# Second attention: a bank of its own for projections, one bank of values by 256 columns, context in quarters

## The reference, cut to what matters

```python
x = x + _L0_xattn_ref(_layernorm(x), ctx_1024, ...)
x = x + _L0_ffn_ref(_layernorm(x), ...)
x = x + _L1_xattn_ref(_layernorm(x), ctx_1024, mask, Wq, Wkv, Wo)   # the stage that changes
x = x + _L1_ffn_ref(_layernorm(x), ...)

def _L1_xattn_ref(x, context, mask, Wq, Wkv, Wo):     # x 4x512x256, context 4x1024x256
    q = (x @ Wq).reshape(B, N, H, D).transpose(0, 2, 1, 3)            # H = 4 heads of D = 64
    kv = (context @ Wkv).reshape(B, M, 2, H, D).transpose(2, 0, 3, 1, 4)
    k, v = (kv[0], kv[1])
    attn = jnp.einsum('bhnd,bhmd->bhnm', q, k) * SCALE
    attn = jnp.where(mask[:, None, :, :], attn, -jnp.inf)
    attn = jax.nn.softmax(attn, axis=-1)
    out = jnp.einsum('bhnm,bhmd->bhnd', attn, v)
    return out.transpose(0, 2, 1, 3).reshape(B, N, C) @ Wo
```

## Time and profile before

| | |
|---|---|
| median of 3 runs | 1119.8 us (1118.17 to 1120.81) |
| the profiled execution | 1110.64 us, of which the span of its instructions is 1108.3 us |
| second attention, from its first scores to the last projection | 474.17 to 786.90 us of the span |
| TensorE matmuls in the four batches | 57.6, 67.6, 67.6, 53.6 us busy of 72.3, 80.3, 79.6, 59.3 us |
| all matmuls / VectorE / ScalarE / GpSimd over the span | 82% / 57% / 47% / 38% |

### The profile page before, as it was taken

How to read it: one execution, slowest core, us unless ns; L and a number is a source line. 1 busy time by engine, 2 the same in 40 slices (tenths; PEclk the granted TensorE clock), 3 DMA queues, 4 the chain that set the end, 5 groups by cost and what they waited for, 6 DMA issues and landing times. The chain is left out here.

```text
span 1108.3 us, 19621 instructions
## 1 busy us (share of the span) xinstructions
PE 914.0 (82%) x6248; PEld 805.5 (73%) x6249; DVE 626.6 (57%) x1352; ACT 516.5 (47%) x1073; POOL 424.6 (38%) x344
## 2 busy tenths in 40 slices
PE   0589989975899991277887888898777999999996
PEld 0378979864799991256776776687656999999995
DVE  2365355148455557556766766769585544445443
ACT  1343324125344441147656656657564555545552
POOL 0454334000455541424424425413005555555543
PEclk9989999897899996598998998999879999999999
DMA  5342110026466655301001001000594766666663
GB/s 172 108 159 76 38 38 1 1 66 234 158 228 227 228 198 167 114 22 38 18 3 58 20 1 39 1 25 1 164 351 143 211 198 190 198 209 203 195 182 60
DMA packets 66417, 131.45 MB, mean 119 GB/s; under 512 B 7696, under 2 KB 50064, under 8 KB 61232
## 3 DMA queue, kind: packets, MB, share of 16 engines
q1 hardware_dynamic: 53872, 110.13, 29.0%
q0 software_dynamic: 12480, 20.48, 8.2%
HBM read 108.95 MB, written 21.64 MB: 118 GB/s over the span
## 5 line engine op out<-in xcount | busy, mean ns | idle before, releaser
L1555 PEld LDWEIGHTS d_hps<-d_xg_t,d_xw 128*128 128x128 f32 x1248 | 146.8, 194 | 3.8 <-DVE d_xg_t L1737 2.4
L1555 PE MATMUL d_hps<-d_xg_t,d_xw 128*128 128x128 f32 x1248 | 147.4, 277 | 1.9 <-DVE d_xg_t L1737 1.9
L1464 ACT ACTIVATE x<-d_hps,b 128x128 f32<-128x128 f32 x312 | 89.2, 368 | 120.8 <-PE d_hps L1555 120.8
L668 POOL TENSOR_SCALAR c_prob<-c_prob,c_rinv 128x1024 f32<-128x1024 f32 x64 | 72.3, 1129 | 181.6 <-DVE c_rinv L1052 181.6
L1565 PE MATMUL d_yps<-d_w,d_hid_hi 128*128 x312 | 115.5, 402 | 3.5 <-DVE d_hid_lo L1746 3.5
L1059 DVE TENSOR_TENSOR c_pt_lo<-c_tp,c_pt_hi 128x512 fp32r<-128x512 f32 x128 | 83.9, 686 | 46.0 <-ACT c_pt_hi L930 45.2
L1390 POOL DMA_INDIRECT out_x<-d_y,d_take_slot x39 | 68.8, 1765 | 101.8 <-DVE d_y L1774 65.2
L930 ACT ACTIVATE c_pt_hi<-c_tp 128x512 fp32r<-128x512 f32 x128 | 71.5, 595 | 61.6 <-PE c_tp L761 60.7
L761 PE MATMUL c_tp<-const,c_prob 128*128 128x128 f32 x512 | 74.4, 285 | 31.0 <-DVE c_q_lo L1029 10.5
L761 PEld LDWEIGHTS c_tp<-const,c_prob 128*128 128x128 f32 x512 | 58.0, 145 | 47.3 <-issue 41.5
L1568 PE MATMUL d_yps<-d_w,d_hid_lo 128*128 x312 | 81.2, 281 | 0.0
(11 more groups left out here) (318 smaller groups left out, 2221.2 us busy)
## 6 DMA issues: line engine op xcount, KB each, us to landing
d_xw<-in_w SPq DMA_DIRECT2D x39, 1024.0 KB
b_w<-in_w SPq DMA_DIRECT2D x47, 512.0 KB, 7.9
d_w<-in_w SPq DMA_DIRECT2D x8, 1024.0 KB, 11.8
a_raw<-in_ctx_t SPq DMA_DIRECT2D x4, 1024.0 KB, 5.3
a_raw<-in_ctx SPq DMA_DIRECT2D x4, 1024.0 KB, 5.3
ybuf<-a_zero SPq DMA_DIRECT2D x2, 2048.0 KB, 13.9
b_ysum<-ybuf SPq DMA_DIRECT2D x8, 512.0 KB, 8.1
c_ctx_t<-in_ctx_t SPq DMA_DIRECT2D x7, 512.0 KB, 3.8
```

The costliest lines, as they stand in the source:

```text
L668: nc.gpsimd.tensor_scalar(prob[w][:], prob[w][:], rinv[:, w:w + 1], 1.0, ALU.mult, ALU.mult).then_inc(s["prob_ready"], 1)
L1464: op = nc.scalar.activation(hid[q][:, h * FH + c, :], src[:, c, :], ACT.Gelu_apprx_tanh, bias=b1[:, ds(e, 1), h * FH + c])
L1555: mm = nc.tensor.matmul(hps[j % 2][h][:, c * P:(c + 1) * P], w1[j % WL][:, k, at:at + P], xg_t[j % 2][:, k, :], start=(k == 0), stop=(k == ...
```

## The change

- A bank of its own, `xb`, takes all projections inside the batches. To make room, `av0` and `av1` become one bank `av`, with 256 columns for each side. So each block of values is one sum of its own: `head_part` and `head_sum` work on 256 columns and there are 8 of them in a batch instead of 4, and each block of values waits for the head sum of the block before (`att_ready`).
- As there is one projection bank instead of two, each projection waits for the low part of the one before. The second one of a period is put after the values, before the turn of side 1.
- VectorE takes both maxima first, ScalarE both exponentials before high_parts(u-1, 1).
- Values of blocks 5, 6 and 7 (block n of the code, by pair of heads, pair of tiles and side) run in periods 0 and 1 of the next batch, as before; the first block of a batch is in u = 3. The output projection of batch b-1 moves from u = 3 to u = 4, its halves on both sides of the values. For odd batches the first block of head outputs goes to `att_odd`, as the projection of the batch before reads `att_t` later.
- The context comes in four pieces of 128x512, with a DMA, a `ctx_high` and a `ctx_low` each: two at the end of u = 3 and two at the end of u = 5. Three of the four x_norm stand at the end of u = 4 without a context copy before them.
- Before the first batch, k_proj(0, 0) goes to `xb` and no longer waits for the low part of x.

The diff, cut (of TensorE's new order u = 0 to 2, 4 and 5 are shown, of ScalarE's u = 5, of VectorE's u = 6; each old order is told above):

```diff
-        av = [ps(f"av{q}", [P, S]) for q in range(2)]
+        xb = ps("xb", [P, S])
+        av = ps("av", [P, S])
...
+                    for p in range(PIECES):
+                        sp.wait_ge(s["ctx_lo"], p + 1 if b == 1 and p < 2 else PIECES * b + p - 1)
+                        load_ctx(b, p)
...
-                    pe.wait_ge(s["pt_lo"], unit(b, hp * TB + pair * 2 + 1, side) * 2 + 4)
-                    if pair == 0:
-                        if hp:
-                            pe.wait_ge(s["att_ready"], b * H + side + 2)
+                    pe.wait_ge(s["pt_lo"], unit(b, hp * TB + pair * 2 + 1, side) * 2 + 2)
+                    if b * 8 + n:
+                        pe.wait_ge(s["att_ready"], b * 8 + n)
...
+                pe.wait_ge(s["w_lo"], 1)
+                pe.wait_ge(s["ctx_lo"], 2)
+                k_proj(0, 0, xb)
+                pe.wait_ge(s["ctx_lo"], 4)
+                pe.wait_ge(s["xn_lo"], 1)
+                k_proj(0, 1, tp[0])
...
+                    scores(b, 0)
+                    k_proj(1, 0, xb)
+                    if before:
+                        turn(b - 1, 7, 0)
+                        values(b - 1, 5)
+                    pe.wait_ge(s["k_lo"], b * 4 + 3)
+                    k_proj(1, 1, xb)
+                    if before:
+                        turn(b - 1, 7, 1)
+
+                    scores(b, 1)
+                    pe.wait_ge(s["k_lo"], b * 4 + 4)
+                    q_proj(1, xb)
+                    turn(b, 0, 0)
+                    if before:
+                        values(b - 1, 6)
+                    turn(b, 0, 1)
+                    if before:
+                        values(b - 1, 7)
+
+                    scores(b, 2)
+                    pe.wait_ge(s["q_lo"], b * KD + 2)
+                    v_proj(0)
+                    turn(b, 1, 0)
+                    pe.wait_ge(s["v_lo"], b * 4 + 1)
+                    v_proj(1)
+                    turn(b, 1, 1)
+                    pe.wait_ge(s["v_lo"], b * 4 + 2)
+                    v_proj(2)
...
+                    scores(b, 4)
+                    if before:
+                        pe.wait_ge(s["wo_in"], 16)
+                        pe.wait_ge(s["att_ready"], b * 8)
+                        project(b - 1, 0, xb)
+                    turn(b, 3, 0)
+                    values(b, 1)
+                    if before:
+                        pe.wait_ge(s["x_ready"], b * 2 - 1)
+                        project(b - 1, 1, xb)
+                    turn(b, 3, 1)
+
+                    scores(b, 5)
+                    if more:
+                        if before:
+                            pe.wait_ge(s["x_ready"], b * 2)
+                        pe.wait_ge(s["xn_ready"], b * TB + 2 * TB)
+                        turn_x(0, xb)
+                    turn(b, 4, 0)
+                    values(b, 2)
+                    if more:
+                        pe.wait_ge(s["xn_lo"], b * KD + KD + 1)
+                        turn_x(1, xb)
+                    turn(b, 4, 1)
...
+                def high_and_exp(b, u):
+                    if u:
+                        high_parts(b, u - 1, 0)
+                    elif b:
+                        high_parts(b - 1, 7, 0)
+                    exponentials(b, u, 0)
+                    exponentials(b, u, 1)
...
+                    if more:
+                        x_high(b + 1, 0, xb)
+                    high_and_exp(b, 5)
+                    head_part(b, 2)
+                    if more:
+                        x_high(b + 1, 1, xb)
+                    high_parts(b, 4, 1)
+                    if more:
+                        ctx_high(b + 1, 2)
+                        ctx_high(b + 1, 3)
...
+                    both_maxima(b, 6)
+                    if more:
+                        k_low(b + 1, 0, 0, xb)
+                    low_and_inverse(b, 6)
+                    if more:
+                        k_low(b + 1, 0, 1, xb)
+                    head_sum(b, 3)
+                    low_parts(b, 5, 1)
```

More of the change, by code:

```diff
@@ L749, in scores, with turn @@
                     mm.then_inc(s["qk_done"], 1)
-                def turn(b, u, side, free):
+                def turn(b, u, side):
                     n = unit(b, u, side)
@@ L792, in batch @@
+                pe.wait_ge(s["xn_lo"], 1)
+                k_proj(0, 1, tp[0])
+                pe.wait_ge(s["w_lo"], 2)
+                pe.wait_ge(s["xn_lo"], 2)
+                q_proj(0, tp[1])
+                for b in range(B):
+                    before, more = b > 0, b < B - 1
                     scores(b, 0)
-                    for half in range(2):
-                        bank_free(b, 0, half)
-                        k_proj(b, 1, half)
-                    k1 = [(s["k_lo"], b * 4 + 3 + half) for half in range(2)]
+                    k_proj(1, 0, xb)
@@ L854, in batch @@
-                    turn(b, 5, 0, [(s["k_lo"], b * 4 + 5 + half) for half in range(2)] if more else NONE)
-                    values(b, 6)
-                    turn(b, 5, 1, NONE)
+                        pe.wait_ge(s["xn_lo"], b * KD + 2 * KD)
+                        pe.wait_ge(s["ctx_lo"], b * PIECES + PIECES + 2)
+                        k_proj(0, 0, xb)
+                    turn(b, 5, 0)
+                    values(b, 3)
+                    if more:
+                        pe.wait_ge(s["k_lo"], b * 4 + 5)
+                        pe.wait_ge(s["ctx_lo"], b * PIECES + 2 * PIECES)
+                        k_proj(0, 1, xb)
@@ L870, in _ @@
-                for half in range(2):
-                    pe.wait_ge(s["xn_lo"], half + 1)
-                    k_proj(0, 0, half)
-                pe.wait_ge(s["w_lo"], 2)
-                pe.wait_ge(s["k_lo"], 1)
-                q_proj(0, 0)
-                batch(0, False, True)
-                pe.wait_ge(s["wo_in"], 16)
-                for b in range(1, B - 1):
-                    batch(b, True, True)
-                batch(B - 1, True, False)
-                turn(B - 1, 7, 0, NONE)
-                values(B - 1, 8)
@@ L883, in _ @@
-                turn(B - 1, 7, 1, NONE)
-                values(B - 1, 9)
-                values(B - 1, 10)
-                pe.wait_ge(s["att_ready"], B * H + 1)
-                for half in range(2):
-                    pe.wait_ge(s["pt_lo"], B * UP * 4 + 1 + half)
-                    project(B - 1, half)
+                        pe.wait_ge(s["k_lo"], b * 4 + 6)
+                        q_proj(0, xb)
+                    turn(b, 6, 0)
+                    values(b, 4)
+                    turn(b, 6, 1)
@@ L997, in _ @@
                 for k in range(KD):
[L998 to L1008 removed]
+                    x_high(0, k, tp[k])
@@ L1152, in _ @@
                 for k in range(KD):
-                    x_low(0, k)
-                k_low(0, 0)
-                q_low(0, 0)
-                batch(0, False, True)
-                for b in range(1, B - 1):
-                    batch(b, True, True)
-                batch(B - 1, True, False)
-                for side in range(2):
-                    low_parts(B - 1, 7, side)
-                for h in (2, 3):
-                    head_sum(B - 1, h)
-                for half in range(2):
-                    add_projection(B - 1, half)
+                    x_low(0, k, tp[k])
```

524 lines of the change are left out of this document (254 added, 270 removed).

## The result

The changed kernel takes 1080.27 us (median of 4 runs, 1078.31 to 1080.48) against 1118.99 us for the kernel before on the same chip: a ratio of 0.965, 95% interval 0.963 to 0.967. That is 38.7 us less; forecast were 37, and 1082.8 us.

The account below looks back on a forecast made before the run. TensorE's own work plus its waits bounds the second attention. Terms -2.6 - 12.0 - 13.2 - 11.5 - 1.4 + 0.8 = -39.9, cut to -37: 1119.8 - 37 = 1082.8 us, range 1070 to 1100.

Parts of the forecast that it names:

- The bound: Second attention: TensorE's own work bounds the stage, plus 12.7 us of batch 1 in which it waits; floor 61.7 us.
- The periods of batch 1: Batch 1 laid out period by period from prices of one plain period: 67.1 us against 80.3, -13.2.
- The gain in u = 5: u = 5 of batch 1: without the 3.5 us x_norm stall, clock stays 1.00; 7.0 us, before 13.9: -6.9.
- Batches 0, 2, 3: Other batches in this order: 60.3 against 72.3 us (-12.0), 68.1 against 79.6 (-11.5), 57.9 against 59.3 (-1.4).
- The 1.0 us of batch 2's u = 0 through the statistics: Batch statistics, ending u = 7 on VectorE, hold up both maxima and first k_low: u = 0 1.0 us longer.
- Before batch 0 and the tail: First k projection no longer waits for the low part of x: -2.6 us; tail waits as u = 1: +0.8.
- The crossings: Layout drops crossings: 0.1 us given back for each of 32 periods, so -39.9 becomes -37.
- A rule against the change: TensorE may not write a bank while another engine reads it, so u = 1's 1.2 us cannot be won back.
- (a): All projections share one bank; uncovered way out keeps u = 0, 2, 3, 6 long: 25 us gain, 1095; chance 0.15.
- (b): TensorE reaches its floor in the batches: 5 us less in three batches, 1068; chance 0.12.
- (c): Many short waits lower TensorE's clock; at 20% of the stage the kernel is at 1132; chance 0.03.
- (d): No change: x_norm and the bank waits were hidden behind another chain; chance 0.02.

Follow-up runs that it names:

- the mixed order with the head copy: Changed kernel, old order of maxima and exponentials outside u=4, u=5 of first three batches, both maxima first and head copy between exponentials in u=1: 1065.34 us, 0.9541.

## Why the prediction was right, point by point

**The bound.** TensorE's work plus its waits: right. The split of the sum was not: batch 1 has 3.7 us of waits left (the four rows above) where 5.4 were priced, and its work, priced at 61.7 us, is 63.7 us busy. The two misses, 1.7 too much and 2.0 too little, nearly cancel. A part of both can be a way of counting, since the prices run from start to start, and the end of a piece that stands before a wait is counted with the wait.

**The periods of batch 1.** u = 0: 8.3 priced, 8.2 measured. u = 1: 10.0, 10.2. u = 2: 9.8, 9.6. u = 3 and 4: 16.8, 16.8. u = 5: 7.0, 7.0. u = 6: 8.4, 8.5. u = 7: 6.8, 7.1. The sum was 67.1 and is 67.4. The gain in u = 5 had two parts, the stall and the clock. With the context out of the way u = 5 lost 5.3 us and had full clock, so that step is shown, with 2.7 us for the stall and 2.6 for the clock.

**Batches 0, 2, 3.** Priced 60.3, 68.1, 57.9; measured 60.6, 68.4, 58.0. The 1.0 us of batch 2's u = 0 through the statistics is 0.9, and moving them took it away. The old order of maxima takes it away too. Batch 0 came out right by luck. The prediction took batch 1 less 11.3 us of work, plus bare waits of 2.0 for k_low, 1.5 for q_low and 1.1 for the second v_low. That keeps the 1.2 us wait for a head sum, which batch 0 does not have, and adds to a v_low wait that was in the sum already. By periods this is about 7.5, 10.9 and 13.2 us for u = 1, u = 2 and the pair u = 3 and 4; measured are 7.2, 10.2 and 14.0. TensorE waits 2.3 us for k_low and never for q_low inside the batch, but 1.7 us for low parts of the turned probabilities. Nor did the prediction see that 0.75 in u = 5 was not the only low clock: u = 1 of batch 0 before ran at 0.83, after a wait of 2.6 us for a maximum, and 2.9 of the 11.6 us gained in batch 0 lie in that period.

**Before batch 0 and the tail.** -2.6 and +0.8 priced; -2.7 and +0.9 measured. The first is right in size and in the wait it names. But the first key projection did not start near 462, 10 us after the Wkv load, as I had it. It starts 11.5 us after the load, when the low part of the weights is done. ScalarE comes to the weights 0.8 us later than before, since its third context piece waits 1.5 us for its DMA, and VectorE's subtraction took 1.23 us before and 2.00 now. So the start is 1.9 us earlier, not 3.5, and yet worth 2.7, because the way from there to the first scores is 0.8 us shorter as well: the matmuls stand 0.43 us apart for 4.0 us instead of 5.7, and 0.23 after that. That the term held is luck, two errors that cancel. In the tail the size held, and the waits are four of 3.7 us in sum (two of them for head sums) against two of 3.2.

**The crossings.** 3 us were given back for what a layout by hand drops. Without them the sum, 39.9, would have been 1.1 over the 38.8 measured; with them it is 1.8 under. The allowance was too large: prices read as distances from start to start hold the crossings already.

**A rule against the change.** The bank of values, priced at 1.2 us in u = 1, cost 0.9. But the rule named there was not what held it: with the head copy between the exponentials TensorE no longer waits in u = 1, on the same one bank. The rule itself was not tried: the copy is out of the bank before the values start. The step named the right queue (the head copy behind both exponentials) and then drew the wrong limit from the bank.

**The rivals.** (a), the projection chain, did not come: the way out lies beside turn and values in u = 0, 6 and 7 and leaves 2.1 us of waits for the low part of v in u = 2 and 3. (b), TensorE at its floor of 61.7 us, was not reached: the mixed order with the head copy brings batch 1 to 65.7. (c), the slower clock: it is 1.00 in the batches, although TensorE waits five times in batch 1. But the mechanism exists here: 2.4 us of waiting in u = 7 of the kernel with only the order (clock 0.85), 4.1 us in u = 6 with the context late (0.79), and in u = 2 of batch 0 with the shared bank and the old order 0.84 after no wait over 1.5 us. The first two kernels are the two slower than before; the third lost 1.5 us by it. (d) is ruled out.

What I took for part of the gain and was not: the new order of maxima and exponentials. The layout had it in every period, so it priced the kernel rightly, but I never laid out the bank with the old order. That is 2.4 us better as it ran and about 3.9 at the full clock, and with the new order kept only in u = 4 and 5, 6.9.

## What to carry to other kernels

Where several engines hand tiles round in a fixed order, read start-to-start distances from one undisturbed period and lay the new order out with them; here that gave each of seven windows within 0.3 us. When an edit has several parts, lay out each part alone as well: the shared bank needed no new order, and the order without the bank lost 11.7 us. Here a copy that fed the busiest engine paid in front of the long instruction of its queue (1.1 us in u = 1), and a copy of data that arrives by DMA paid behind x_norm (9.5 us in three periods).

## What the runs showed of the hardware

- TensorE's clock is at its full or at its half level. The period with the 3.5 us stall had full clock up to 1.3 us after the stall and half for 6.8 us. Periods with single waits of 2.0, 2.4 and 4.1 us were at 0.84, 0.85 and 0.79, and the one with 4.1 us took 6.6 us more than before. Periods with waits of 1.8 to 1.9 us were at 1.00 in u = 5 of two kernels (x_norm behind context pieces, old order with the bank), and with x_norm ahead of the context copy at 1.00 in one batch and 0.83 in another. The same instructions with the same waits, 1.5 us at most, ran at 0.84 in one kernel and 1.00 in another. So the length of the longest wait does not settle it, and what does is left open here.
- VectorE's subtractions of two SBUF operands stretch when GpSimd is busy. In all twelve profiled executions the low part of Wq (128x512), which took 1.52 to 2.83 us, ended 0.54 to 0.55 us after the end of the GpSimd instruction beside it, and the low part of Wkv (128x1024), which took 1.22 to 2.35 us, 1.08 to 1.10 us after one. Before (two rows) and now (two rows):

```profile
460.89 3.33 POOL L650 TENSOR_TENSOR c_ctx_lo<-c_prob,c_ctx_hi 128x1024 fp32r<-128x1024 f32 x1
461.94 2.82 DVE L1151 TENSOR_TENSOR c_wq_lo<-c_prob,c_wq_hi 128x512 fp32r<-128x512 f32 x1
466.60 1.90 POOL L673 TENSOR_SCALAR c_minf<-c_mask 128x1024 bf16<-128x1024 uint8 x1
467.52 1.52 DVE L1130 TENSOR_TENSOR c_wq_lo<-c_prob,c_wq_hi 128x512 fp32r<-128x512 f32 x1
```

  They look as if they did their work only after GpSimd was done. The GpSimd subtraction of 128x1024 took 2.35 us in the same trace, and 3.33 here, where VectorE's subtraction of Wkv lay over its start.
- Copies of half the width: 0.38 us for 64x256 against 0.60 for 64x512, and the head sum 0.43 against 0.69. I had taken 0.37 for the copy.
